# Layer-0 scores of the next block moved inside the first step of a block, between parts of the query

## The reference

```python
# layer 0: one head of width 512, masked, residual
q = x @ Wq.T + bq;  k = y @ Wk.T + bk;  v = y @ Wv.T + bv
scores = where(mask == 0, -1e9, q @ k.T)
x = softmax(scores) @ v + x
# layer 1: 16 heads of width 32, residual, layer norm
Q = x @ W1q.T + b;  K = y @ W1k.T + b;  V = y @ W1v.T + b
attn = softmax(Q_h @ K_h.T / sqrt(32))          # for each head h
z = concat_h(attn @ V_h) @ Wo.T + bo + x
out = (z - mean(z)) / sqrt(var(z) + 1e-5) * gamma + beta
```

## Time and profile before

| | us |
|---|---|
| three executions | 391.55, 393.39, 395.25 |
| median | 393.39 |
| profiled execution, its time | 394.95 |
| its span, first to last instruction | 393.0 |

### The profile page before, as it was taken

One profiled execution on the slowest core, in us unless ns is written; L12 is line 12 of the kernel. 1 busy time (PEld: TensorE's weight loads), 2 busy tenths in 40 slices (PEclk: granted clock), 3 DMA queues, 4 the chain that ended last, 5 costly groups with the idle time before them and its releaser, 6 DMA issues.

```text
span 393.0 us, 11993 instructions
## 1 busy us (share of the span) xinstructions
PE 377.4 (96%) x4860; PEld 286.7 (73%) x4860; DVE 295.1 (75%) x711; ACT 245.9 (63%) x749; POOL 222.0 (56%) x245
## 2 busy tenths in 40 slices
PE   8999998899999999999999999999999999799894
PEld 7878956577777787777777777778777777577663
DVE  0446587568867997799977996799778997457886
ACT  2343778765588666866487558856686648556820
POOL 0520655435647764785578664785478647733541
PEclk9999999999999999999999999999999999899999
DMA  8937410530042322522152224222243113322022
GB/s 309 392 125 231 123 39 20 189 107 4 18 157 98 98 71 65 176 94 64 44 177 77 85 72 155 99 98 72 83 147 118 30 57 92 138 97 71 19 107 107
DMA packets 22461, 42.52 MB, mean 108 GB/s; under 512 B 3685, under 2 KB 5221, under 8 KB 22279
## 3 DMA queue, kind: packets, MB, share of 16 engines
q1 hardware_dynamic: 21866, 41.06, 31.8%
q10 hardware_dynamic: 540, 0.69, 0.5%
HBM read 26.49 MB, written 8.39 MB: 89 GB/s over the span
## 4 chain that ended last, share of the span: by engine, by line
PE 82%; ACT 9%; DMA 4%; DVE 3%; issue 1%; SPq 0%; DVEq 0%
PE ps_q L1035 21%; PE ps_out L1124 21%; PE ps_t L1063 11%; PE ps_s L1049 7%; PE ps_pv L1099 6%; PE ps_out L995 5%; ACT prob L563 3%; ACT y L600 2%; PE ps_s L961 2%; DMA pt<-pt 2%; ACT pt L574 1%; PE ps_s L1142 1%; PE ps_s L974 1%; DMA raw<-in_w0k 1%; ACT q L524 1%
## 5 line engine op out<-in xcount | busy, mean ns | idle before, releaser
L418 POOL TENSOR_TENSOR prob<-prob,rc 128x308 f32<-128x308 f32 x128 | 91.9, 725 | 113.5 <-DVE rc L785 112.8
L563 ACT ACTIVATE prob<-ps_s,mx 128x77 f32<-128x77 f32 x512 | 120.5, 334 | 3.5 <-DVE mx L776 3.3
L574 ACT ACTIVATE pt<-ps_t 122x512 f32<-122x512 f32 (+2 forms) x93 | 55.6, 598 | 56.1 <-PE ps_t L1063 53.0
L783 DVE TENSOR_REDUCE sm<-prob 128x4 f32<-128x308 f32 x128 | 59.5, 465 | 25.6 <-ACT prob L563 25.1
L776 DVE TENSOR_REDUCE mx<-ps_s 128x4 f32<-128x308 f32 x128 | 53.7, 465 | 17.8 <-PE ps_s L1049 17.8
L1063 PE MATMUL ps_t<-ident,prob 128*122 128x128 f32 (+1 forms) x372 | 58.3, 279 | 1.7 <-ACT pt L574 1.6
L392 POOL TENSOR_TENSOR x_l<-x_raw,x_h 128x512 fp32r<-128x512 f32 x32 | 44.4, 1390 | 21.0 <-ACT x_h L506 10.8
L1063 PEld LDWEIGHTS ps_t<-ident,prob 128*122 128x122 f32 (+1 forms) x372 | 46.1, 153 | 13.0 <-issue 3.7
L1035 PE MATMUL ps_q<-x_h,wq_h 128*128 128x512 f32 x128 | 53.4, 417 | 0.0
L1035 PE MATMUL ps_q<-x_h,wq_l 128*128 128x512 f32 x128 | 53.0, 414 | 0.0
L1049 PEld LDWEIGHTS ps_s<-k1T,q 32*64 32x64 f32 x2048 | 26.2, 133 | 28.0 <-issue 15.9
(11 more groups left out here) (134 smaller groups left out, 616.9 us busy)
## 6 DMA issues: line engine op xcount, KB each, us to landing
x_raw<-in_xT SPq DMA_DIRECT2D x14, 512.0 KB, 4.4
y<-in_x SPq DMA_DIRECT2D x28, 256.0 KB, 3.0
out<-y SPq DMA_DIRECT2D x28, 256.0 KB, 2.3
pt<-pt SPq DMA_DIRECT2D x31, 90.0 KB, 2.6
pt<-pt SPq DMA_DIRECT2D x31, 64.0 KB, 2.0
mask_sb<-in_mask SPq DMA_DIRECT2D x8, 154.0 KB, 4.7
raw<-in_w0q SPq DMA_DIRECT2D x4, 256.0 KB, 5.3
x_raw<-in_xT SPq DMA_DIRECT2D x1, 1024.0 KB, 7.7
```

Source lines behind the costliest of these rows:

```text
L418: nc.gpsimd.tensor_tensor(ap, ap, wide(rc[:, k % 2, h], KEYS), ALU.mult).then_inc(prob_done, 1)
L563: e = nc.scalar.activation(prob[:, k % 2, t, h], ps_s[:, h, t * KEYS:(t + 1) * KEYS], ACT.Exp, bias=mx[:, k % 2, h, t:t + 1])
L574: nc.scalar.activation(pt[0:n, c], ps_t[0:n, :], ACT.Copy).then_inc(pt_ready, 1)
L783: nc.vector.reduce_sum(sm[:, k % 2, h], prob[:, k % 2, :, h], AX_X).then_inc(sum_done, 1)
```

## The change

In a step with g = 0, `layer0(i, b + 1)` goes between `transposes(k-1, 1)` and query products 5 to 9, instead of behind query product 13. Step 0 keeps its place (there the call stands under `if k == 0`). In the last block, whose step has no layer 0 to do, the three groups of output products are issued together behind query product 13; for the other blocks the removed `part` calls did nothing.

```diff
@@ -1239,7 +1239,8 @@
                 if g == 0:
-                    part(0)
+                    if k > 0:
+                        layer0(i, b + 1)
                     query(i, k + 1, 5, 10)
                 elif g == 3:
                     part(1)
@@ -1247,17 +1248,18 @@
                     part(0)
                 transposes(i, k - 1, 2)
                 if g == 0:
-                    part(1)
                     query(i, k + 1, 10, QUERY)
+                    if b == LAST:
+                        for n in range(3):
+                            part(n)
                 else:
                     query(i, k + 1, 5, 10)
                 if type(i) is int and k == 1:
                     fold(1, 2, CH)
                 if g == 0:
-                    part(2)
                     if k == 0:
                         project(bank[5:7], raw1, ctxT_sb, mm_v1T, [ld_w1v, ld_w1v], 1, CH)
-                    layer0(i, b + 1)
+                        layer0(i, b + 1)
                     if k == 0:
```

## The result

| | before | after |
|---|---|---|
| median, us | 393.44 (391.55 to 395.25, 4 executions) | 409.31 (406.99 to 411.68, 4 executions) |
| profiled execution, its time | 394.95 | 406.99 |
| its span | 393.0 | 405.1 |

The ratio is 1.040, 95% interval 1.032 to 1.049: 15.9 us slower by the medians, 12.1 by the two spans.

The account below looks back on a forecast made before the run. TensorE, busy 96% of the 393.0 us span, was taken as the bound. Waits of 11.8 us plus clock falls of 5.8 gave 17.6 on the profiled 394.95, 412.5, or 411.0 us on the median, range 402 to 415.

Parts of the forecast that it names:

- The new waits: Scores behind the context wait for ACT's q, 2.1 us in each of five steps and 1.25 at k = 4.
- k = 4: Step 4, without a normalise in ACT's queue: scores wait 1.25 us for q.
- 0 us, at worst some tenths: Layer 0's own wait for x_raw, closest at k = 4: none expected, some tenths in a slow transfer.
- k = 24: Step 24: wait of 2.1 us for q, with PE's unexplained pause inside layer 0 either kept or gone.
- The steps behind: Following steps: the delayed work behind scores late by the same 2.1 us adds nothing.
- k = 28: Last block's step, output products grouped: context still waits for the pt<-pt transfer; bounds 0 to -3.5 us, taken as 0.
- The clock: Behind the new waits: granted clock falls, 1.44 us each, bounds 0 to 8.6; four falls taken, 5.8 us.
- the rule that was weighed there: Skill page on PE's clock warns only of longer gaps: clock would hold, 11.8 us alone; forecast went by k = 28 instead.
- Wait without clock: Rival: the six waits come but the clock holds, 393.4 + 11.8 = 405.2 us; few or no falls, chance 0.26.
- Absorbed on ACT: Rival: q doesn't wait for the third transposes' chain, or ACT makes up the delay; 393.4 us, chance 0.07 including mostly absorbed.
- More than the sum: Rival: late results or x_raw waits cost each of six steps another 0.5 to 1 us; 415 to 418, chance 0.07.

Follow-up runs that it names:

- e1: Changed kernel with layer 0 directly behind the third transposes, in front of query products 10 to 13, still inside the query: 395.34 us, ratio 1.000.
- e2: Changed kernel with layer 0 halved: tiles 0 and 1 at the new place, tiles 2 and 3 at the old place: 398.16 us, ratio 1.010.
- e4: Changed kernel with ScalarE doing the exponentials of heads 2 and 3 before evicting the third transposes (g = 0, from k = 4): 396.22 us, ratio 1.005.
- e3: Changed kernel with PE's new waits filled by recomputing layer-0 tiles (1.7 us, 1.1 at k = 4): 406.66 us, ratio 1.031.
- e8: Changed kernel unaltered, measured once more beside two filled versions: 408.16 us, ratio 1.034 to the kernel before.
- e7: Kernel before with only ScalarE's order changed, exponentials of heads 2 and 3 before the third eviction where g = 0: 393.61 us, ratio 1.000.
- e5: Kernel before with only the k = 28 output products grouped behind the query, layer 0 at its old place: 393.79 us, ratio 0.999.
- e6: Kernel before with the last block's 1 MB row load issued one step later, behind both pt<-pt moves of k = 28: 392.33 us, ratio 0.996.
- e9: Changed kernel with waits filled by repeated layer-0 tiles (1.7 us, 1.1 at k = 4), rerun beside the unfilled changed kernel: 406.16 us, ratio 1.029.
- e10: Changed kernel with one repeated layer-0 tile (0.57 us) as filling in each of the six steps: 405.46 us, ratio 1.027.
- The filled kernels: Changed kernel with PE's new waits filled by useless layer-0 products: 406.16 us with the full filling, 405.46 us with one tile.

## Why the prediction was right

The forecast was 411.0 us in 402 to 415; measured were 409.31 and, again, 408.16. The direction, the cause and the size of the five main waits were right. That the total came so near is in part luck: the term of the clock was taken too large, and the terms that were left out, x_raw and a pause at k = 4, a pause at k = 12, made up for it. Over the kernel before beside it the loss was 15.9 and 13.0 us, where the sum said 17.6. By its steps:

- **The new waits.** Right in place, cause and size. 2.13 us were worked out for k = 8, and the step is 10.88 - 8.76 = 2.12 us longer; k = 16 and 20 likewise. e1, e2 and e4 each move or shorten one thing in the chain and the wait follows it; e3 shows that it is a wait. Two errors of 0.2 us cancelled: the third transposes came 2.48 us later after the step's start, not 2.28 (126.77 - 119.51 against 121.40 - 116.62), since the five query products behind layer 0 took 1.36 us where they had taken 1.16 (why is open), and ACT's chain from the eviction to the end of q was 3.57 us long, not 3.76 (130.34 - 126.77 against 125.16 - 121.40). Before, the normalise hadn't followed the exponentials by ACT's order alone, as I had read it. Its operand nb was ready only at 123.73, just in front of 123.77, by this line of the kernel before:

```profile
123.57 0.16 DVE L835 SCALAR_TENSOR_TENSOR nb<-both,rs 128x2 f32<-128x2 f32 x1 [1.49 <-POOL rs L426]
```

  In the changed kernel nb was there 2.3 us before ACT came to it. PE's own work in the step took 0.3 us longer, so the idle time in front of the scores was 1.72 us and not the 2.06 that were set beside the 2.0 of k = 28.
- **k = 4.** 1.25 us predicted, 1.23 measured as the wait for q, but the step grew by 4.3. What failed is the line "0 us, at worst some tenths" for x_raw: layer 0 waited 0.8 us, and behind its first 28 records came a pause of 1.51 us that no wait explains. By the starts, layer 0 began 0.8 us late and lasted 1.8 us longer than at k = 8; the other 0.4 us are the later transposes and a later start of the scores behind q. In e8 the step grew by 3.2 us, with a pause of 0.42.

```profile
76.95 0.73 PE L995 MATMUL ps_out<-a,x_raw 128*32 128x77 f32 x28 [0.76 <-DMA x_raw<-in_xT]
...
79.19 1.93 PE L995 MATMUL ps_out<-a,x_raw 128*32 128x77 f32 x100 [1.51 <-issue]
```

  The 0.7 us of margin came from a profile in which step 3 took 9.36 us, held up by a slow move of the start; it took 8.1 to 8.2 us in nine of the eleven profiles that followed (9.6 to 9.7 in e2 and e7), and layer 0 then comes sooner, here by 1.4 us (scores of k = 4 at 73.05, before at 74.42), while the load comes only 0.8 us sooner and takes 5.2 us to land. With layer 0 in front of the third transposes it waited for x_raw at k = 4 in all seven profiles, 0.25 to 1.0 us. A margin was read off one execution, in a stretch that varies.
- **k = 24.** 2.1 predicted, and 10.88 us measured, 1.5 more than before; the pause that the kernel before had there (0.33 us) is gone, in e8 too. A pause came at k = 12 instead, 0.71 us here and 0.99 in e8, which the sum did not have.
- **The steps behind.** The sum took them as unchanged. In the four profiles with all of layer 0 at its old place (before, e5, e6, e7) steps 5, 9, 17 and 21 are longer than 11.72 us by 1.6 to 3.5 us in sum, with pauses in them; in the changed kernel none is, but for the falls of the clock. This gives back a part of the waits and is at least a part of why e2, e8, e9 and e10 came out under their expectations.
- **k = 28.** 0 predicted, and e5 says 0 for that half of the diff. In the profiles the step is 0.8 us shorter and the next 0.95: the transfer was 0.3 us less late and the clock held. Both vary between executions: in e8 the wait was 2.2 us and the clock fell.
- **The clock.** The mechanism was right, the size was not: "I take four falls, 5.8 us". The price of one was right (1.44 predicted from k = 28; 1.5 to 1.6 at k = 9 and 13), their number was not: one behind the five long waits in each of two profiled executions, where four were taken. The filled kernels put the whole at 2.0 to 2.7 us by their medians, with intervals that overlap. A single gap of 2 us with a fall behind it had been read as what such gaps do, when they do it now and then; and at k = 28 too it fell in four of the eleven profiles that have that wait (before, e1, e8, e10). The lowest mean clock of the ten executions of the changed kernel is 0.986; by an estimate from it and the 3.41 us of a fall that is room for three falls in all, the one at k = 28 and that of the last microseconds included. The kernel before has a fall at k = 28 in its one profile and none there in e5 and e7, which leave layer 0 and that load at their old places; my sum counted that one profile as the normal state.

On the rule that was weighed there (the Trainium skill, TensorE: Matmul & The Clock Gate, "Why this matters for your kernels"): by it the clock would have held behind gaps as short as these. It mostly did, but not always: it fell behind waits of 1.7 us (k = 8; k = 12 in e8). Of the two numbers, 0 by the page and my 5.8, the 1.5 us of a profiled execution and the 2.0 to 2.7 us of the filled kernels' medians are nearer to the page's.

- **The rivals.** "Wait without clock" (405.2) is nearer to the profiled execution (406.99, one fall) than my number and further from the first median, 409.31. Counted over the kernel before beside it, its 11.8 us are nearer to e8's 13.0 than my 17.6, and further from the first 15.9. So the two are about even, where I gave this one 0.26. "Absorbed on ACT" is what e4 makes true by another order on ACT. "More than the sum" had one true part, x_raw at k = 4.

## What to carry to other kernels

Work that is moved within the order of the busiest engine isn't free: list what another engine starts from each place that the moved work now stands in front of, and compare that engine's chain with the cover that is left behind it. Here 4.08 us of cover against 3.8 of chain became 1.80, and moving the same work by one place, from in front of a producer to behind it, was worth some 13 us (e1 against e8, each over the kernel before beside it). If the place must stay, shorten the chain: let the other engine do in front of the late input what doesn't need it.

## What the runs showed of the hardware that was not expected

- A fall of the granted clock behind PE's idle time didn't come each time that the idle time was there. Behind waits of 1.7 us it fell once in five in each of two profiled executions (k = 8; k = 12). Six waits of at most 1.2 us (e10) and five of 0.7 us (e2) went without. The wait of k = 28 had a fall behind it in four profiles, at 1.84 to 2.16 us, and none in seven, at 0.71 to 2.20 us. So the length of one gap doesn't settle it; in e9 a wait of 0.76 us and a pause of 1.27 us close behind it were followed by a fall. Each of these falls lasted 3.41 us, and where it lay in one step it cost about 1.5 us of it.
- Runs of very short products pause without a wait: 1.51 and 0.71 us inside layer 0 in the changed kernel (k = 4 and k = 12), 0.33 in the kernel before. The two kernels of which there are two profiles each paused in the same steps both times, with other lengths: the changed one (e8: 0.42 and 0.99 us), and the filled one at k = 4 and k = 20 (0.45 and 0.83 us in e3, 1.27 and 1.10 in e9). Before, e6 and e7, in which PE's order is the same, share the long steps 9 and 17, but not the pause of k = 24. So the place goes in part with the order of the instructions, and the length varies; whether that makes the scatter of 4 us wasn't tried. Step 9 took 12.38, 12.39, 12.83 and 12.83 us in the four profiles that have all of layer 0 right in front of context and scores (before, e7, e5, e6), and 11.72 to 11.73 where layer 0 stands further ahead, is shorter there or a wait follows it, and the clock holds (e2, e3, e4, e8 to e10). The cause of the pauses stays open.
- A 64 KB move inside SBUF that usually lands in 2.0 us took 5.6 us behind a 1 MB load issued 2.8 us before it (4.9 in e5, 4.3 in e7; e6: 1.9 us without the load in front). The 90 KB move between the two took 4.7 us instead of 2.6.
